# Second attention of a four-layer block: sums stay with heads on partitions, denominators of two units collected, inverted and spread by DMA

## The chip, the cores and the metric

The kernel runs on one core of one Trainium2 chip. The metric is the device time of one execution in microseconds (us), the median of repeated runs. The engines are TensorE (PE: matrix products, transposes through an identity matrix), VectorE (DVE), ScalarE (ACT), GpSimd (POOL) and SyncE (SP), whose queue issues every DMA of this kernel.

## The reference

`x` has 4 batches of 1024 tokens with 256 channels; `ctx` has 77 tokens a batch. Four residual steps follow each other; the change lies in the third.

```python
x = x + tanh(g_xattn[0]) * L0_xattn(layernorm(x), ctx, ...)
x = x + tanh(g_ffn[0])   * L0_ffn(layernorm(x), ...)
x = x + tanh(g_xattn[1]) * L1_xattn(ctx, ctx, layernorm(x), mask, Wv, Wk, Wq, Wo, bo)
x = x + tanh(g_ffn[1])   * L1_ffn(layernorm(x), ...)

def L1_xattn(values, keys, queries, mask, Wv, Wk, Wq, Wo, bo):   # 16 heads of 16 channels
    v, k, q = values @ Wv.T, keys @ Wk.T, queries @ Wq.T         # per head
    energy = where(mask, einsum('bqhd,bkhd->bhqk', q, k), -1e20)
    attn = softmax(energy / sqrt(16), axis=-1)                   # over 77 keys
    out = einsum('bhqk,bkhd->bqhd', attn, v).reshape(N, 1024, 256)
    return out @ Wo.T + bo
```

## The kernel before

The second attention works in 16 **units** `u`: batch `u // 4`, and four heads `4 * (u % 4)` to `4 * (u % 4) + 3`. Each unit has two **steps** of 512 queries, numbered `m = 2 * u + q`, so 32 steps. A step of PE is `scores1(m)`: for each of four heads a product for the row maxima of the next unit (L1278, L1280), then the scores with keys on partitions (L1313, L1314). Then come `values1(m - 1)` (L1322), `max_transposes1(m + 2)` (L1293) and `out_transposes1(m - 2)` (L1331). In the steps m = 2, 4, ..., 16 four transposes of normalised input (L1257) stand among the scores.

`values1` leaves 128 rows in one bank of PSUM: for each of four heads, 32 rows, of which the first 16 are the head's output channels and row 16 is the sum of the exponentials, the softmax denominator. ACT copies the bank to one of two buffers `Oe` (L933), `out_transposes1` turns it so that queries are on partitions, and DVE (`normalise1`) takes the reciprocal of the denominators (L1891) and multiplies (L1894) into `On`. After the 32 steps PE turns `On` back, 512 queries at a time (`transposes1`, L1356), ACT copies that to `OnT` (L957), and PE projects it with `wo1` (L1375). There are eight such chunks `c`. DVE adds each to `x` (`x3_batch`, L1925), takes the statistics of the next normalisation (L1931), and normalises (L1703); then the fourth step's transposes begin (L1388).

Beside it: ACT takes the exponentials of the scores (L945, four a step) and stages the negated maxima (L927); POOL copies those into the query stack (`max_rows1`, L746), which `scores1` of two steps later waits for, and after the steps 20, 23, 26 and 29 adds a bias to one batch of `x` (L763). DVE reduces the maxima (L1872).

SP's queue loads the query stack of each unit three units ahead: `load_x_stack(u)`, six DMAs of 16 partitions with 4 rows of 2 KB each (L541). It waits for the scores of unit u - 3, whose buffer it takes, and the maxima of unit u are the first to read it, from the first product of step 2u - 2. After the loads of u = 2, 5, 7, 9 and 11 it writes chunks of the split input to memory (`write_parts`, L533, 768 KB each), which later loads read. PE waits for ACT (`s_e1`, `s_oc`), for DVE (`s_mr`) and for the loads (`s_xs`); nothing else orders the work but each engine's own list.

Of the kernel before, what the change touches and what calls it, by code (L numbers as in the profile page):

```python
# [11 lines left out]
F32 = mybir.dt.float32  # L12
# [26 lines left out]
def build_program(nc, ins, out):  # L39
    ctx = ExitStack()  # L40
    with ctx:
# [131 lines left out]
        s_fs = sem("ffn0_setup_product")  # L173
        s_fsc = sem("ffn0_setup_copied")
# [36 lines left out]
        Oe = R2f[:, 6100:7124].rearrange("p (u n) -> p u n", u=2)  # L211
# [8 lines left out]
        On = R1[:, :].rearrange("p (i c) -> p i c", i=NT)  # L220
        OnT = R3f[:, 0:2048].rearrange("p (u j n) -> p u j n", u=2, j=2)
        Mn = small[:, 464:496].bitcast(BF16).rearrange("p (u q j) -> p u q j", u=2, q=8)
        rc1 = small[:, 528:544].rearrange("p (q j) -> p q j", q=4)
# [27 lines left out]
        s_ot1 = sem("out1_transposed")  # L251
        s_rc = sem("out1_recip")
        s_on = sem("out1_normalised")
        s_gb = sem("gated_bias")
        s_xb = sem("bias_added")
# [20 lines left out]

        QP = nc.dram_tensor("q_parts", (3, B * C, S), BF16).ap()
# [74 lines left out]
        s_gb2 = sem("gated_bias2")  # L352
        s_xb2 = sem("bias2_added")
# [9 lines left out]
        s_kf = sem("k_copied")  # L363
# [124 lines left out]
        def _(sp):  # L488
# [57 lines left out]
            write_parts(1)  # L546
            for u in range(UNITS):
                b = u // 4
                if u % 4 == 0:
                    sp.wait_ge(s_pw[0], 16 * (b + 1))  # L550
                    sp.wait_ge(s_pw[1], 16 * (b + 1))
                load_x_stack(u)
                for c in WRITES.get(u, ()):
                    write_parts(c)
            sp.wait_ge(s_ksc, 6)
# [3 lines left out]
                         allow_slow_non_contiguous=True).then_inc(s_qgl, 16)  # L559
            def write_qk(dst, c, filled, written):  # L560
# [120 lines left out]
        def _(pool):  # L681
# [100 lines left out]
            pool.tensor_scalar(bp2[:, :], bp2[:, :], gates[:, 3:4], None, ALU.mult).then_inc(s_gb2, 1)  # L782
# [30 lines left out]
            pool.wait_ge(s_gb2, 1)  # L813
            pool.wait_ge(s_xn, 4 * NC)
            for b in range(B):
                xs = X[:, TB * b:TB * b + TB, :]
                pool.tensor_tensor(xs, xs, bp2[:, :].unsqueeze(1).to_broadcast([P, TB, C]), ALU.add).then_inc(s_xb2, 1)
# [6 lines left out]
        def _(act):  # L824
# [25 lines left out]
            for j in range(2):  # L850
                act.wait_ge(s_fs, j + 1)
                act.copy(BWt[:, j, 0:NB16], bank(4 + j)[:, 0:NB16]).then_inc(s_fsc, 1)
            act.wait_ge(s_fs, 3)
            act.copy(BW[0:97, :], bank(6)[0:97, 0:C]).then_inc(s_fsc, 1)
# [97 lines left out]

            for c in range(NC):
                act.wait_ge(s_onT, c + 1)
                if c >= 2:
                    act.wait_ge(s_wo, c - 1)
                act.copy(OnT[:, c % 2], bank(2 * (c % 2), 2).rearrange("p (j t) -> p j t", j=2)).then_inc(s_onc, 1)  # L957
# [89 lines left out]
            for c in range(NC):  # L1047
                n = NC + c
                act.wait_ge(s_onT, n + 1)
# [6 lines left out]
        def _(pe):  # L1056
# [73 lines left out]
            for j in range(2):  # L1130
# [3 lines left out]
                mm.then_inc(s_fs, 1)  # L1134
            pe.wait_ge(s_fsc, 2)
            for j in range(2):
                mm = pe.matmul(bank(6)[0:97, 0:C], BWt[:, j, :], wdT[:, j, :], start=(j == 0), stop=(j == 1))
            mm.then_inc(s_fs, 1)
            pe.wait_ge(s_x1, 4 * B)
            pe.wait_ge(s_fsc, 3)  # L1140
# [185 lines left out]
            def out_transposes1(m):  # L1326
                pe.wait_ge(s_oc, m + 1)
                if m >= 1:
                    pe.wait_ge(s_on, m)
                for i in range(4):  # L1330
                    mm = pe.transpose(bank(3)[:, P * i:P * i + P], Oe[:, m % 2, P * i:P * i + P], identF[:, :])  # L1331
                mm.then_inc(s_ot1, 1)

# [4 lines left out]
            for m in range(2 * UNITS):  # L1338
# [864 lines left out]
```

## Time and profile before

| | |
|---|---|
| median of 3 runs | 1333.91 us (1333.17 to 1338.76) |
| the profiled execution | 1333.7 us, span 1332.0 us |
| PE busy | 1215.1 us, 91% of the span |
| DVE, ACT, POOL busy | 1000.7, 835.3, 227.5 us |
| DMA | 92.55 MB, mean 69 GB/s |
| the 32 steps of the second attention | from about 230 to 383 us of the span |
| its projection | 383 to 421 us |

PE's clock is shown as a share of full speed. The rows further down are of three kinds: stretches of time with the busy time of each engine; the chain of work that ended last, followed back from the end, where an item on the chain delays everything behind it; and timelines. A matmul's printed duration contains its passage through the array, so matmuls overlap; the chain shows what each adds.

### The profile page before, as it was taken

Reading aid. Unit: us, or ns where it says so; the run is one execution under the profiler, and the core shown is the slowest. Engines: PE = TensorE matmul, PEld = TensorE weight load, DVE = VectorE, ACT = ScalarE, POOL = GpSimd, SP = SyncE. Lnnn points to the kernel's source line nnn. Section 1 sums busy time; section 2 is a strip of 40 time slices with the busy share of each in tenths; the row PEclk is TensorE's granted clock in tenths of the full one; section 3 lists DMA queues with packets and bytes.
Section 4 is the critical chain, followed back from the end, with each engine's and each line's share of the span. In section 5 each row is a group of like instructions: output and inputs, shape, how many; then the busy total and the mean of one; then the engine's idle time right before and its main releaser. Section 6 shows DMA issues by size and latency. Waiting matters only on the chain.

```text
span 1332.0 us, 26359 instructions
## 1 busy us (share of the span) xinstructions
PE 1215.1 (91%) x10562; PEld 565.5 (42%) x10562; DVE 1000.7 (75%) x1491; ACT 835.3 (63%) x1484; POOL 227.5 (17%) x176
## 2 busy tenths in 40 slices
PE   4989974999999898879999999999999999999988
PEld 3566762555567455343233232332232333333247
DVE  4895695665536758368999999999999999999602
ACT  1224573777742742115887878887788877888861
POOL 2130124554741423710000000000000000000000
PEclk9878985999999999888999999999999999999989
DMA  6100027557500334722323443144332543233003
GB/s 189 26 1 15 1 31 137 121 108 136 96 1 1 119 119 135 134 35 48 56 62 64 87 72 63 47 82 84 56 68 56 87 78 59 56 70 50 2 1 126
DMA packets 78825, 92.55 MB, mean 69 GB/s; under 512 B 15210, under 2 KB 53356, under 8 KB 78704
## 3 DMA queue, kind: packets, MB, share of 16 engines
q1 hardware_dynamic: 78704, 90.87, 33.7%
q8 instruction: 84, 1.38, 0.5%
q14 instruction: 37, 0.30, 0.1%
HBM read 67.02 MB, written 23.80 MB: 68 GB/s over the span
## 4 chain that ended last, share of the span: by engine, by line
PE 60%; DVE 27%; ACT 5%; issue 2%; SPq 2%; DMA 2%; POOL 1%; DVEq 0%; ACTq 0%; POOLq 0%
DVE sm L2093 19%; PE ps L1560 10%; PE ps L1551 9%; PE ps L1532 6%; ACT W L1022 3%; PE ps L1322 2%; PE ps L1670 2%; PE ps L1416 2%; PE ps L1313 2%; PE ps L1314 2%; PE ps L1375 2%; PE ps L1542 1%; PE ps L1280 1%; PE ps L1278 1%; PE ps L1331 1%
## 5 line engine op out<-in xcount | busy, mean ns | idle before, releaser
L1022 ACT ACTIVATE W<-ps 128x512 f32<-128x512 f32 x1024 | 534.8, 605 | 140.6 <-PE ps L1560 136.7
L2093 DVE TENSOR_REDUCE sm<-ps 128x1 f32<-128x1024 f32 x512 | 599.3, 1217 | 29.7 <-PE ps L1532 26.3
L1560 PE MATMUL ps<-R 99*32 99x512 bf16 x4096 | 319.2, 384 | 5.5 <-ACT W L1022 3.2
L1551 PE MATMUL ps<-W,R 128*32 128x512 f32 x2048 | 265.5, 594 | 0.7 <-ACT W L1022 0.7
L1560 PEld LDWEIGHTS ps<-R 99*32 99x32 bf16 x4096 | 86.1, 94 | 225.2 <-ACT W L1022 167.0
L803 POOL COPY R<-R 128x512 f32<-128x512 f32 x16 | 9.7, 613 | 629.5 <-PE ps L1551 625.9
L1532 PE MATMUL ps<-R 50*128 50x512 bf16 x512 | 89.9, 390 | 17.7 <-DVE sm L2093 15.0
L1532 PE MATMUL ps<-KM,R 50*128 50x512 bf16 x512 | 87.3, 384 | 9.6 <-DVE sm L2093 6.6
L945 ACT ACTIVATE R<-ps 77x512 f32<-77x512 f32 x128 | 75.1, 592 | 23.5 <-PE ps L1314 14.2
L1551 PEld LDWEIGHTS ps<-W,R 128*32 128x32 f32 x2048 | 63.0, 111 | 42.2 <-ACT W L1022 1.4
L1872 DVE TENSOR_REDUCE small<-ps 128x4 bf16<-128x308 f32 x128 | 57.5, 472 | 23.2 <-PE ps L1280 23.1
L746 POOL COPY R<-R 4x2048 bf16<-4x2048 bf16 x32 | 60.5, 1890 | 60.1 <-ACT R L927 54.1
L1532 PEld LDWEIGHTS ps<-R 50*128 50x128 bf16 x512 | 22.2, 93 | 97.0 <-DVE sm L2093 47.2
L1532 PEld LDWEIGHTS ps<-KM,R 50*128 50x128 bf16 x512 | 22.0, 93 | 89.7 <-issue 48.4
L1416 PE MATMUL ps<-R,W 128*128 128x512 f32 x128 | 57.9, 595 | 0.0
L1703 DVE TENSOR_SCALAR XN<-X,mv,rstd 128x256 f32<-128x256 f32 x128 | 46.7, 431 | 9.8 <-PE ps L1092 9.6
L1313 PE MATMUL ps<-R 100*77 100x512 bf16 x128 | 49.0, 383 | 0.0
L1314 PE MATMUL ps<-R 77*77 77x512 bf16 x128 | 48.6, 380 | 0.0
L1891 DVE RECIPROCAL small<-ps 128x16 f32<-128x16 f32 x32 | 8.2, 257 | 47.1 <-PE ps L1331 47.1
L1278 PE MATMUL ps<-R 77*128 77x308 bf16 x128 | 38.7, 303 | 4.1 <-DMA R<-x_parts 4.0
L2104 DVE RECIPROCAL sm<-ps 128x16 f32<-128x16 f32 x32 | 8.2, 257 | 44.7 <-PE ps L1542 44.7
L1280 PEld LDWEIGHTS ps<-R 96*128 96x128 bf16 x512 | 35.0, 100 | 12.9
(262 smaller groups left out, 1576.0 us busy)
## 6 DMA issues: line engine op xcount, KB each, us to landing
R<-x_parts SPq DMA_DIRECT2D x96, 128.0 KB, 4.8
R<-q_parts SPq DMA_DIRECT2D x192, 64.0 KB
R<-q_parts SPq DMA_DIRECT2D x96, 128.0 KB
R<-k_parts SPq DMA_DIRECT2D x96, 128.0 KB
x_parts<-R SPq DMA_DIRECT2D x8, 768.0 KB, 7.0
q_parts<-R SPq DMA_DIRECT2D x24, 256.0 KB, 2.6
k_parts<-R SPq DMA_DIRECT2D x24, 256.0 KB, 2.6
X<-in_x SPq DMA_DIRECT2D x4, 1024.0 KB, 9.8
```

What stands on the lines that cost most here:

```text
L746: pool.tensor_copy(Xs[m // 2 % 3][SR:SR1, :, 512 * (m % 2):512 * (m % 2) + 512], mrow1[:, m % 2].unsqueeze(1).to_broadcast([4, 4, 512])).t ...
L945: act.activation(P1[:, m % 2, j, :], score_bank1(n)[0:KX, :], ACT.Exp, scale=0.25).then_inc(s_e1, 1)
L1022: act.activation(PR[:, s % 2, h, :], third_bank("score", 64 * u + n), ACT.Exp, scale=0.25).then_inc(s_sfree, 1)
L1278: pe.matmul(o, mb1[:, P * q:P * q + P], I4, start=True, stop=False, skip_group_check=True)
L1313: pe.matmul(o, K1s[:, 4 * hg + j, KX * b:KX * b + KX], Xs[u % 3][:, j, t], start=True, stop=False)
L1314: pe.matmul(o, I4[:, 0:KX], mb1[:, t], start=False, stop=True).then_inc(s_sc, 1)
L1416: mm = pe.matmul(o[:, 512 * j:512 * j + 512], wqkv[:, i, C * kind + P * j:C * kind + P * j + P], XNT3[:, i, 512 * c:512 * c + 512], start= ...
L1532: mm = pe.matmul(pl[:, 512 * i:512 * i + 512], QMH[j][h][v, P * q:P * q + P], KM[j][v, h, :], start=True, stop=True)
L1551: mm = pe.matmul(bank(7)[32 * h:32 * h + 32, :], VST[j][:, k, h, :], PR[:, s % 2, h, :], start=(k == 0), stop=(k == TB - 1))
L1560: mm = pe.matmul(o[32 * c:32 * c + 32, :], KST[j][0:MAX_ROW + 1, h, t:t + 32], QST[j][0:MAX_ROW + 1, h, 512 * (s // 8):512 * (s // 8) + 51 ...
L1872: dve.tensor_reduce(Mn[:, u % 2, q, :], bank(n % 2)[:, 0:4 * KX].rearrange("p (j n) -> p j n", j=4), AX, ALU.max, negate=True).then_inc(s_ ...
L2093: dve.tensor_reduce(MX[:, half, h, q:q + 1], bank(2 * ((p + 1) % 2), 2), AX, ALU.max).then_inc(s_tfree, 1)
```

## The change

The sums keep heads on partitions from `values1` to the projection. `out_transposes1`, `normalise1`, `transposes1` and ACT's copies to `OnT` are gone. In their place SP's queue moves things:

- `sort_out1(m)`: ACT's copy in `Oe` (now four buffers) is sorted by four DMAs of 16 partitions x 2 KB into `OT1`, where channels are on partitions in the order that the projection reads, and a fifth DMA puts the four rows of denominators into memory (`DN1`).
- For each **pair** `k` of units (2k and 2k + 1), and each half q: `load_sums1` brings the eight denominator rows back spread over 128 partitions, DVE inverts them (`invert_sums1`), `store_factors1` writes them, and `spread_factors1` brings each row back on 16 partitions. DVE multiplies `OT1` by that (`divide_pair1`). The pairs 5, 6 and 7 are divided behind the loop, the last two between the additions of `x3_batch`.
- The projection reads `OT1` directly and waits for the divided pairs (`s_nd1`).

Some semaphores of other stages are merged or dropped; no instruction of those stages changes.

```diff
-        Oe = R2f[:, 6100:7124].rearrange("p (u n) -> p u n", u=2)
+        Oe = [R2f[:, a:a + 512] for a in (6100, 6612, 7168, 7680)]
...
+        OT1 = R1[:, :].rearrange("p (j b t) -> p j b t", j=2, b=B)
+        Rd1 = R2f[:, 5946:6074].rearrange("p (u q n) -> p u q n", u=2, q=2)
+        Den1 = W[:, 2152:3176].rearrange("p (q n) -> p q n", q=2)
...
+            def sort_out1(m):
+                u, q = m // 2, m % 2
+                b, rows, j = u // 4, 64 * (u % 2), u // 2 % 2
+                sp.wait_ge(s_oc, m + 1)
+                if m >= 2:
+                    sp.wait_ge(s_od1[q], 80 * (m // 2))
+                for h in range(4):
+                    v = slice(rows + 16 * h, rows + 16 * h + 16)
+                    sp.dma_start(OT1[v, j, b, 512 * q:512 * q + 512],
+                                 Oe[m % 4][32 * h:32 * h + 16, :]).then_inc(s_od1[q], 16)
+                sp.dma_start(DN1[u // 2 % 2, q, 4 * (u % 2):4 * (u % 2) + 4],
+                             Oe[m % 4][16:P:32, :]).then_inc(s_od1[q], 16)
+            def load_sums1(k):
+                for q in range(2):
+                    sp.wait_ge(s_od1[q], 80 * (2 * k + 2))
+                    sp.dma_start(Rd1[:, k % 2, q, :],
+                                 DN1[k % 2, q].rearrange("g (a n) -> (g a) n", a=16)).then_inc(s_dd1[q], 16)
+            def store_factors1(k):
+                for q in range(2):
+                    sp.wait_ge(s_ri1, 2 * k + q + 1)
+                    sp.dma_start(DR1[k % 2, q].rearrange("g (a n) -> (g a) n", a=16),
+                                 Rd1[:, k % 2, q, :]).then_inc(s_dd1[q], 16)
+            def spread_factors1(k):
+                for q in range(2):
+                    sp.wait_ge(s_dd1[q], 32 * k + 32 + (16 if k == UNITS // 2 - 2 else 0))
+                    if k >= 1:
+                        sp.wait_ge(s_nd1, 2 * (k - 1) + q + 1)
+                    sp.dma_start(Den1[:, q, :], DR1[k % 2, q].unsqueeze(1).to_broadcast([8, 16, 512])
+                                 ).then_inc(s_db1[q], 16)
+            def store_sums1(u):
+                for m in (2 * u, 2 * u + 1):
+                    sort_out1(m)
+                if u >= 3 and u % 2 == 1:
+                    store_factors1((u - 3) // 2)
+                if u >= 4 and u % 2 == 0:
+                    spread_factors1((u - 4) // 2)
+                if u >= 2 and u % 2 == 0:
+                    load_sums1((u - 2) // 2)
             for u in range(UNITS):
...
+                if u >= 3:
+                    store_sums1(u - 3)
...
+            for u in range(UNITS - 3, UNITS):
+                store_sums1(u)
+            load_sums1(UNITS // 2 - 1)
+            spread_factors1(UNITS // 2 - 2)
+            store_factors1(UNITS // 2 - 1)
+            spread_factors1(UNITS // 2 - 1)
...
             def copy_out1(m):
                 act.wait_ge(s_pv, m + 1)
-                if m >= 2:
-                    act.wait_ge(s_ot1, m - 1)
-                act.copy(Oe[:, m % 2], bank(7)).then_inc(s_oc, 1)
+                if m >= 4:
+                    act.wait_ge(s_od1[m % 2], 80 * (m // 2 - 1))
+                act.copy(Oe[m % 4], bank(7)).then_inc(s_oc, 1)
...
-                if m >= 2:
-                    out_transposes1(m - 2)
             values1(2 * UNITS - 1)
-            out_transposes1(2 * UNITS - 2)
-            out_transposes1(2 * UNITS - 1)
...
             for c in range(NC):
-                if c + 1 < NC:
-                    transposes1(c + 1)
-                pe.wait_ge(s_onc, c + 1)
+                b, q = c // 2, c % 2
+                pe.wait_ge(s_nd1, 4 * b + 3 + q)
...
-                        mm = pe.matmul(o, OnT[:, c % 2, j, P * i:P * i + P], wo1[:, j, :],
+                        mm = pe.matmul(o, OT1[:, j, b, 512 * q + P * i:512 * q + P * i + P], wo1[:, j, :],
...
+            def invert_sums1(k):
+                for q in range(2):
+                    dve.wait_ge(s_dd1[q], 32 * k + 16)
+                    dve.reciprocal(Rd1[:, k % 2, q, :], Rd1[:, k % 2, q, :]).then_inc(s_ri1, 1)
+            def divide_pair1(k, q):
+                dve.wait_ge(s_db1[q], 16 * (k + 1))
+                o = OT1[:, k % 2, k // 2, 512 * q:512 * q + 512]
+                dve.tensor_tensor(o, o, Den1[:, q, :], ALU.mult).then_inc(s_nd1, 1)
...
-                if m >= 2:
-                    normalise1(m - 2)
+                if m >= 9 and m % 4 == 1:
+                    invert_sums1((m - 9) // 4)
+                if m >= 13 and m % 4 in (1, 2):
+                    divide_pair1((m - 13) // 4, m % 4 - 1)
```

How the instructions stand, at three places. First SP's queue, before: two units of loads (`x_parts` is the split input in memory, `R` any of the large buffers).

```order
L541 DMA R<-x_parts 16x4x1024 [waits scores1]
L541 DMA R<-x_parts 16x4x1024 x5
L533 DMA x_parts<-R 128x6x512 [waits part_l]
L541 DMA R<-x_parts 16x4x1024 [waits scores1]
L541 DMA R<-x_parts 16x4x1024 x5
```

The same place of SP's queue with the change, for one unit in which a chunk is written and a pair's factors are spread (`sum_rows` is `DN1`, `sum_factors` is `DR1`).

```order
L541 DMA R<-x_parts 16x4x1024 [waits scores1]
L541 DMA R<-x_parts 16x4x1024 x5
L533 DMA x_parts<-R 128x6x512 [waits part_l]
L555 DMA R<-R 16x512 [waits out1_sorted0,out1_copied]
L555 DMA R<-R 16x512 x3
L557 DMA sum_rows<-R 4x512
L555 DMA R<-R 16x512 [waits out1_sorted1,out1_copied]
L555 DMA R<-R 16x512 x3
L557 DMA sum_rows<-R 4x512
L577 DMA W<-sum_factors 128x1x512 [waits out1_divided,out1_factors_moved0]
L577 DMA W<-sum_factors 128x1x512 [waits out1_divided,out1_factors_moved1]
L563 DMA R<-sum_rows 128x32 [waits out1_sorted0]
```

Between one unit's loads and the next's the queue now holds ten sorting DMAs and either four (here) or two for the factors; the next loads stand behind all of them, and behind their waits. Second, PE behind the last scores, before (`XN` is the normalised input).

```order
L1322 MATMUL ps<-R 32x512 x4
L1331 MATMUL ps<-identF,R 128x128 x8
L1356 MATMUL ps<-identF,R 128x128 x8
L1363 MATMUL ps<-sm 128x2
L1356 MATMUL ps<-identF,R 128x128 x8
L1375 MATMUL ps<-wo,R 128x256 x8
```

PE behind the last scores with the change.

```order
L1360 MATMUL ps<-R 77x512
L1368 MATMUL ps<-R 32x512 x8
L1386 MATMUL ps<-sm 128x2
L1398 MATMUL ps<-wo,R 128x256 x64
L1411 MATMUL ps<-identF,XN 128x128 x16
```

All transposes between the last values and the next stage are gone; the 64 products of the projection follow each other. Third, DVE during the projection with the change (L1914 divides, L1909 inverts, L1947 adds to `x`).

```order
L1914 TENSOR_TENSOR R<-R,W 128x512 [waits out1_factors_spread0]
L1914 TENSOR_TENSOR R<-R,W 128x512 [waits out1_factors_spread1]
L1909 RECIPROCAL R<-R 128x32 [waits out1_factors_moved0]
L1909 RECIPROCAL R<-R 128x32 [waits out1_factors_moved1]
L1940 COPY sm<-ps 128x2 [waits q_g_product]
L1947 SCALAR_TENSOR_TENSOR X<-ps,gates,X 128x1024 [waits biases_added,projected] x2
L1909 RECIPROCAL R<-R 128x32 [waits out1_factors_moved0,x3_added]
L1909 RECIPROCAL R<-R 128x32 [waits out1_factors_moved1]
L1914 TENSOR_TENSOR R<-R,W 128x512 [waits out1_factors_spread0]
L1914 TENSOR_TENSOR R<-R,W 128x512 [waits out1_factors_spread1]
L1953 BN_STATS stats<-X 128x6 x8
```

The statistics of the first batch now stand behind the factors of pair 6, which come through the queue above.

## Rows read from the trace of the kernel before

**Rows 1.** Stretches: us, busy (instructions) of PE, PEld, DVE, ACT, POOL, clock, DMA share, GB/s
```profile
320.00:350.00 30.00, 30.00 (x286) 16.33 (x283) 15.40 (x38) 22.88 (x39) 17.76 (x9) 1.00 0.63 115
```

**Rows 2.** Chain that ended last, one step: start us, us, engine, output, line
```profile
339.99 0.99 PE ps L1322 x8
...
341.21 0.59 PE ps L1331 x4
...
342.08 0.22 PE ps L1313
...
344.67 0.99 PE ps L1322 x8
```

**Rows 3.** The same chain earlier, four transposes among the scores
```profile
300.35 0.44 PE ps L1257 x4
```

**Rows 4.** Timeline of ACT, one step: start us, us, line, operation [idle before]
```profile
304.83 2.69 ACT L945 ACTIVATE R<-ps 77x512 f32<-77x512 f32 x4 [0.37 <-PE ps L1314]
307.95 0.58 ACT L933 COPY R<-ps 128x512 f32<-128x512 f32 x1 [0.43 <-PE ps L1322]
308.56 0.58 ACT L927 CAST R<-ps 4x512 bf16<-4x512 f32 x1
```

**Rows 5.** DVE groups of the whole run: busy us, mean ns | idle before
```profile
L1894 DVE TENSOR_TENSOR R<-ps,small 128x256 f32<-128x256 f32 x32 | 13.6, 424 | 1.1
...
L1821 DVE TENSOR_TENSOR R<-R 128x1024 f32<-128x1024 f32 x8 | 9.8, 1226 | 0.3
...
L1891 DVE RECIPROCAL small<-ps 128x16 f32<-128x16 f32 x32 | 8.2, 257 | 47.1 <-PE ps L1331 47.1
```

**Rows 6.** Timeline, SP's queue: one unit's six loads
```profile
306.92 2.65 SPq L541 DMA_DIRECT2D R<-x_parts  x6
```

**Rows 7.** Stretches of half a us: clock, DMA share, GB/s; loads, then a chunk's write
```profile
311.50:312.00 0.50, 1.00 1.13 139
...
324.50:325.00 0.50, 1.00 1.09 385
```

**Rows 8.** Chain that ended last, the stage's first load: first issue, last issue's landing
```profile
212.02 0.32 SPq L541
...
214.26 6.08 DMA R<-x_parts
```

**Rows 9.** Timeline of POOL around one bias addition
```profile
333.01 1.89 POOL L746 COPY R<-R 4x2048 bf16<-4x2048 bf16 x1 [2.77 <-ACT R L927]
334.98 4.52 POOL L763 TENSOR_TENSOR X<-X,bo 128x2048 f32<-128x2048 f32 x1
```

**Rows 10.** Chain that ended last, from the last values product to the next stage
```profile
382.57 0.60 PE ps L1331 x4
...
387.69 3.72 PE ps L1375 x16
...
392.28 3.46 PE ps L1375 x16
...
413.09 1.29 DVE X L1925
...
414.41 2.71 DVE stats L1931 x8
...
417.88 2.35 DVE XN L1703 x7
...
421.56 1.08 PE ps L1388 x8
```

**Rows 11.** DMA issues of the whole run: count, KB each, us from issue to landing
```profile
q_parts<-R SPq DMA_DIRECT2D x24, 256.0 KB, 2.6
```

**Rows 12.** Timeline of POOL and DVE, later in the kernel
```profile
513.99 2.12 POOL L791 TENSOR_TENSOR R<-R 128x1024 bf16<-128x1024 f32 x1 [3.56 <-ACT R L997]
...
514.25 1.87 DVE L2012 TENSOR_TENSOR sm<-sm 128x1 f32<-128x1 f32 x1
...
517.12 0.19 DVE L2017 TENSOR_TENSOR sm<-sm 128x32 f32<-128x32 f32 x1
```

More of the change, by code:

```diff
@@ L250, in build_program @@
         s_oc = sem("out1_copied")
[L251 to L255, printed above, removed]
+        s_od1 = [sem(f"out1_sorted{n}") for n in range(2)]
+        s_dd1 = [sem(f"out1_factors_moved{n}") for n in range(2)]
+        s_db1 = [sem(f"out1_factors_spread{n}") for n in range(2)]
+        s_ri1 = sem("out1_recip")
+        s_nd1 = sem("out1_divided")
+        s_gb = sem("gated_biases")
+        s_xb = sem("biases_added")
         s_onT = sem("heads_transposed")
@@ L275, in score_bank1 @@
             return bank(4 + n % 3)
+        DN1 = nc.dram_tensor("sum_rows1", (2, 2, 8, 512), F32).ap()
+        DR1 = nc.dram_tensor("sum_factors1", (2, 2, 8, 512), F32).ap()
         QP = nc.dram_tensor("q_parts", (3, B * C, S), BF16).ap()
@@ L850, in _ @@
             for j in range(2):
[L851 to L854, printed above, removed]
+                act.wait_ge(s_ks, 6 + j + 1)
+                act.copy(BWt[:, j, 0:NB16], bank(4 + j)[:, 0:NB16]).then_inc(s_ksc, 1)
+            act.wait_ge(s_ks, 6 + 3)
+            act.copy(BW[0:97, :], bank(6)[0:97, 0:C]).then_inc(s_ksc, 1)
             def y_copy(c):
@@ L951, in _ @@
             copy_out1(2 * UNITS - 1)
[L953 to L957, printed above, removed]
             def transpose_copy(c):
@@ L1324, in values1 @@
                 mm.then_inc(s_pv, 1)
[L1326 to L1332, printed above, removed]
             for q in range(2):
@@ L1343, in _ @@
                     max_transposes1(m + 2)
-                if m >= 2:
-                    out_transposes1(m - 2)
             values1(2 * UNITS - 1)
-            out_transposes1(2 * UNITS - 2)
-            out_transposes1(2 * UNITS - 1)
-            def transposes1(c):
-                if c >= 2:
-                    pe.wait_ge(s_onc, c - 1)
-                for j in range(2):
-                    for i in range(4):
-                        mm = pe.transpose(bank(2 * (c % 2) + j)[:, P * i:P * i + P],
-                                          On[:, 4 * c + i, P * j:P * j + P], identF[:, :])
-                mm.then_inc(s_onT, 1)
-            pe.wait_ge(s_on, 2 * UNITS)
-            transposes1(0)
             pe.wait_ge(s_qc, 2)
@@ L1914, in _ @@
                             blk[:, :].unsqueeze(2).to_broadcast([P, 8, 16])).then_inc(s_qc, 1)
-            normalise1(2 * UNITS - 2)
-            normalise1(2 * UNITS - 1)
+            for q in range(2):
+                divide_pair1(UNITS // 2 - 3, q)
+            invert_sums1(UNITS // 2 - 2)
             dve.wait_ge(s_qk, 1)
@@ L1940, in _ @@
                 x3_batch(b)
+                if b == 0:
+                    invert_sums1(UNITS // 2 - 1)
+                    for q in range(2):
+                        divide_pair1(UNITS // 2 - 2, q)
+                if b == 1:
+                    for q in range(2):
+                        divide_pair1(UNITS // 2 - 1, q)
                 if b + 1 < B:
```

46 lines of the change are left out of this document (13 added, 33 removed).

## The prediction

> **What bounds the kernel now.** I read the stretches first, to see which engine is full in the second attention. PE is busy for all of the 30 us, at clock 1.00, its 2.4 GHz level, while DVE has 15.40, ACT 22.88 and the DMA engines a share of 0.63 [rows 1]. The chain then gives a step's length: from one values product to the next 344.67 - 339.99 = 4.68 us, all of it PE, and 0.59 us of that is the output transposes L1331 [rows 2]. So PE sets the pace, and what it loses is gained until another engine or queue takes over. Three come close.
>
> ACT needs 2.69 + 0.58 + 0.58 = 3.85 us a step [rows 4], under the 4.08 us that PE would have left. SP's queue takes 2.65 us for six DMAs, the first one's 0.32 us shorter than the rest [rows 6, 8]; that is a pitch of (2.65 - 0.32) / 5 = 0.466 us. The DMA engines move a unit's loads at 139 GB/s although their share is full, and a chunk's write at 385 [rows 7]: loads of 16 partitions are slow. From the first issue of a unit's loads to their landing it was 214.26 + 6.08 - 212.02 = 8.3 us [rows 8]. A load may start when its buffer's scores are done and is needed two steps and a bit later (values, maxima, transposes: 342.08 - 339.99 less two small products, 1.8 us), so before it has 9.4 + 1.8 - 8.3 = 2.9 us to spare.
>
> **The change part by part.** The sum is made against the profiled execution, 1333.7 us, which lies 0.2 us under the median.
>
> *PE, in the loop.* 30 times L1331 at 0.59 us [rows 2]: at most 17.7 us, a step of 4.68 - 0.59 = 4.09.
>
> *DVE.* 32 reciprocals of 0.257 and 32 products of 0.424 us go, 21.8 us [rows 5]. 16 reciprocals of twice the width and 16 products of 512 columns come; half of the 1024-column product is 0.61 us, and with 0.26 to 0.51 for a reciprocal this is 14 to 18 us. DVE has half of the stretch free [rows 1], so neither counts, as long as DVE does not wait in line. In the loop it inverts a pair six steps after the pair's last step and divides it four steps later. The load of the sums is issued some four and a half steps after that last step and lands 2.6 us later, by the nearest row for a plain transfer [rows 11]; one step is left. Zero, with that step as cover.
>
> *SP's queue.* Per pair of units (four steps): 12 loads, 20 sorting DMAs, 6 for the factors = 38 x 0.466 = 17.7 us, and 18.1 with a chunk's write. Before, four steps took 18.7 us, or 19.5 with two sets of L1257 at 0.44 us (m = 2 to 16) [rows 3]. PE alone would need 16.3 and 17.2. So the queue, and no longer PE, is the floor: the gain is 1.4 us per four steps for three groups (steps 5 to 16) and 1.0 for 2.75 groups (17 to 27), 6.9 us together; before step 5 and behind step 27 the queue is not full, some five steps gain their 0.59, 3.0 us. In-loop gain **9.9 us** in place of 17.7. The bounds for a sorting DMA's issue are those of the rows: 0.32 us (gain near 17) and 0.466; I take the upper one, as all repeated DMAs of one shape have it.
>
> *POOL.* A bias addition stands between two copies of maxima: 1.89 + 0.08 + 4.52 + 0.1 + 1.89 = 8.5 us from the first copy's start to the second's end [rows 9], and PE reads the second's result at 342.08 [rows 2], 9.1 us after that start. At 4.09 us a step that shrinks to 7.9, late by 0.6 three times; at the queue's 4.42 it is 8.6 and hidden. I take 0.5 us lost, between 0 and 1.8.
>
> *The loads behind the queue.* This is the added wait that matters: the next unit's six loads stand behind the sorting DMAs, whose second set waits for ACT's copy of the last step. From the moment the scores are done: the copy is 4.42 + 1.7 us later, then five issues (2.3) and four for the factors (1.9) = 10.3, against 8.8 for two steps. Every second unit's loads are issued 1.5 us late, with two transfers of 256 KB just ahead of them: 0.7 us each at a write's 385 GB/s, 1.9 at a load's 139 [rows 7]. The spare time has shrunk to 8.8 + 1.2 - 8.3 = 1.7 us. So every second load is late by 1.5 + 1.4 - 1.7 = 1.2 us or more: six times, **7 us lost**. The bounds: 0, if sorts and loads slip past each other, and the case below where the engines are full.
>
> For the rate of a sorting DMA the row at 139 GB/s speaks [rows 7]: it too moves 16 partitions x 2 KB, 0.24 us each. The Trainium skill, SBUF — State Buffer, "Door 1: The DMA port swizzle", says that 16 partitions reach only four of sixteen ports, with 104 GB/s measured; the trace's 139 is above it, and by the page's figure a sort would be an estimated 0.32 us, which makes the rival of full engines dearer by 1.3 us per four steps. The Trainium skill, DMA: Bandwidth & Descriptors, "Rules for kernel authors", says of many small transfers to coalesce them, as under 64 KB one pays mostly overhead; these are 32 KB, and the queue's pitch above is such an overhead. Taken as a forecast, that rule leaves nothing of the in-loop gain: 1333.7 - 5 = 1329 us.
>
> *Behind the loop.* From the last values product's end to the next stage's transposes it is 421.56 - 382.57 = 39.0 us [rows 10]. Gone are the two last turns and divisions with a copy, 387.69 - 382.57 = 5.1 us, and seven times 392.28 - 387.69 - 3.72 = 0.87 us of L1356: PE alone gains 11.2. But pairs 6 and 7 now pass through the queue. From the last values: copy 0.8, five issues 2.3, landing 2.6, sums loaded 0.9 + 2.6, factors spread (pair 6 waits for pair 7's sums by the semaphore's count) 0.9 + 2.6: 12.7. DVE then: two divisions 1.3, statistics 2.71 + 0.6, two additions 2.6, two divisions 1.3 (pair 7 is back by then), statistics 3.3, additions 2.6, statistics 3.3, normalisation 2.35, one addition 1.3: 34.0 us. PE, at 3.46 us a chunk, is done with its part by then. Gain 39.0 - 34.0 = **5.0 us**, between 0 (a landing more in the chain) and 11.2.
>
> Sum: 9.9 - 0.5 - 7 + 5.0 = 7.4; 1333.7 - 7.4 = **1326.3 us**.
>
> **The rivals.**
>
> 1. *The DMA engines fill up* (slower). Where the sorts and the spreading run at the loads' rate, four steps need 2 x 5.7 us for the loads (768 KB at 139), 16 x 0.24, 2 x 1.9, and 2.0 for a chunk: 20.9, and 18.9 without the chunk, against 19.5 and 18.7 before. That is 3 x 1.4 + 2.75 x 0.2 = 4.8 us lost, and a late load idles PE while SP waits for the copy that comes late from it, which I put at 2 us a group, 11.5. With 3.0 and 5.0 gained outside: slower by 8.3, **1342 us**. It decides from some 0.16 us a sort on. For it: the full share at 139 GB/s. Against: the queue issues sorts at a fourth of the loads' bytes per us, much of it into gaps (share 0.63).
> 2. *Late loads take the whole in-loop gain* and the tail stays near 3: **1331 us**, no change that can be told.
> 3. *Everything is hidden*: issues of 0.32 us, loads in time; PE's pace: 17.7 - 1.8 + 5 = 20.9, **1313 us**.
> 4. *A division waits for POOL.* A DVE product of one column with both inputs in SBUF took 1.87 us while POOL's product ran, and ended with it; one of 32 columns later took 0.19 [rows 12]. The divisions are of that kind. The one of step 21 comes as the bias addition of 4.52 us starts [rows 9]; with two maxima ahead in the banks (1.4 us) PE would stand 3.1 us: **1329 us**. In the Trainium skill, SBUF — State Buffer, "Who interferes with whom", this is a rule: a DVE instruction with two SBUF inputs contends with a GpSimd instruction that reads SBUF. The trace agrees.
>
> **How the numbers follow.** A measurement can tell about 0.5%, 6.7 us: under 1327.2 is faster, over 1340.6 slower. The forecast (1319 to 1330) has 0.45, of which a quarter lies above 1327.2; rival 3 has 0.13, rival 2 0.17, rival 4 0.05, rival 1 0.20, a tenth of it under 1340.6. Faster: 0.34 + 0.13 = 0.47; slower 0.18; same 0.35. The range of 1314 to 1341 leaves out half of rival 3 and half of rival 1. The forecast's own range is 1319 to 1330.
>
> **What would show it.** Right: PE waits for the x_parts loads in every second unit; steps of some 4.4 us; SP's issues back to back; the stretch from the last values to L1411 at 34 us. The queue term is wrong if L555 is issued at much under 0.4 us. Rival 1 shows as PE waits of several us and a DMA share near 1.0 throughout; rival 4 as one L1914 of over 3 us. The prediction falls if PE's chain still runs unbroken, or if the tail is longer than 39 us.

## The result: slower by 4%, and the profile after

The changed kernel takes **1388.33 us** (1386.12 to 1390.68, 4 runs) against 1334.03 for the kernel before on the same chip: 1.0401 times as long, 95% interval 1.0375 to 1.0427. The forecast was 1326.3, and the range ended at 1341. The profiled execution took 1388.78 us. Some kernels below had executions over 1.5% longer than their fastest; the ratios leave these out, the medians hold all.

First the stretches of the profile after, cut where the granted clock changes; they answer to [rows 1], where PE was full at 1.00. Columns: stretch, then PE, PE's weight loads, DVE, ACT and POOL busy (instructions), granted clock, DMA share, GB/s.

```profile
243.20:279.40 36.20, 33.29 (x320) 17.78 (x317) 19.42 (x44) 28.72 (x51) 23.24 (x17) 1.00 0.75 129
279.40:286.30 6.90, 6.41 (x32) 3.72 (x32) 2.51 (x5) 2.36 (x4) 1.23 (x3) 0.51 0.43 85
286.30:303.30 17.00, 14.25 (x137) 7.41 (x136) 8.79 (x20) 12.58 (x22) 9.69 (x7) 1.00 0.87 162
303.30:310.20 6.90, 4.22 (x24) 2.93 (x25) 0.96 (x2) 1.61 (x3) 0.74 (x1) 0.51 0.73 130
310.20:327.20 17.00, 15.36 (x146) 7.87 (x144) 8.31 (x17) 13.32 (x24) 10.10 (x8) 1.00 0.79 148
327.20:439.60 112.40, 107.50 (x521) 45.54 (x521) 32.93 (x69) 48.28 (x82) 43.31 (x27) 0.50 0.45 92
...
443.30:473.20 29.90, 26.43 (x122) 22.61 (x120) 24.36 (x73) 0.00 (x0) 6.29 (x7) 1.00 0.14 41
```

The clock falls to 0.5, its 1.2 GHz level, three times. Twice it is back after 6.9 us; the third time, from 327.20 on, it stays there to the loop's end, with PE busy for 107.50 of 112.40 us. What comes before each fall stands in the chain of waits (start us, us, what), here for the first one:

```profile
271.10 1.00 PE ps L1368 x8
...
275.27 1.04 PE ps L1368 x8
...
277.64 1.90 POOL R L798
279.54 0.35 issue
279.89 0.42 PE ps L1324
280.31 0.26 PE ps L1326 x4
```

A step of the unbroken stretch takes 275.27 - 271.10 = 4.17 us, against 4.68 before [rows 2]. Then PE stands from 276.49 to 279.89: L1324 opens the next unit's maxima, behind the wait for that unit's stack. The chain names POOL's copy of maxima, but that copy is for the step after this one, and it ended 0.35 us earlier (the item "issue"); the last packet of the unit's loads landed at 279.80. The other two gaps, 300.55 to 305.98 and 325.56 to 331.30, end 0.1 us behind such a landing too (305.89, 331.21). Behind the third a step takes 7.9 us:

```profile
336.94 1.87 PE ps L1368 x8
...
344.84 1.87 PE ps L1368 x8
```

Why the loads are late stands in SP's own queue (start us, us, what; the issues answer to [rows 6]):

```profile
271.34 2.77 SPq L541 DMA_DIRECT2D R<-x_parts  x6
274.21 2.42 SPq L555 DMA_DIRECT2D R<-R  x4
276.68 0.53 SPq L557 DMA_DIRECT2D sum_rows<-R  x1
277.30 3.70 SPq L555 DMA_DIRECT2D R<-R  x4
281.05 0.52 SPq L557 DMA_DIRECT2D sum_rows<-R  x1
281.61 0.91 SPq L569 DMA_DIRECT2D sum_factors<-R  x2
282.56 2.77 SPq L541 DMA_DIRECT2D R<-x_parts  x6
285.38 0.43 SPq L533 DMA_DIRECT2D x_parts<-R  x1
285.90 3.30 SPq L555 DMA_DIRECT2D R<-R  x4
289.25 0.53 SPq L557 DMA_DIRECT2D sum_rows<-R  x1
289.88 2.41 SPq L555 DMA_DIRECT2D R<-R  x4
292.33 0.52 SPq L557 DMA_DIRECT2D sum_rows<-R  x1
292.89 1.65 SPq L577 DMA_DIRECT2D W<-sum_factors  x2
294.58 0.93 SPq L563 DMA_DIRECT2D R<-sum_rows  x2
295.62 0.36 SPq L541 DMA_DIRECT2D R<-x_parts  x1
```

The queue never stands. Four steps take it 295.62 - 271.34 = 24.3 us, PE alone 4 x 4.17 = 16.7, or a little more with L1303 (the four transposes of normalised input in every second step up to 16, L1257 before). Four sorts take 2.4 us, a pitch of 0.63, and here up to 3.7.

**Where the time went.** From the first values product to the end of the last one it was 143.65 us before (238.92 to 382.57) and is 199.58 (240.07 to 439.65): +55.9. The tail fell from 39.0 to 33.6 us (439.65 to 473.24): -5.4. The rest is +1.2 ahead of the loop and +2.2 behind the tail; the sum is 53.9 = 1385.9 - 1332.0, the difference of the two spans. In the loop the gaps are 3.40 + 5.43 + 5.74 = 14.6 us; the long half-clock stretch costs 107.50 x (1 - 4.17 / 7.89) = 50.7 and the two short ones (6.41 + 4.22) x 0.47 = 5.0. Without these 70.3 us the loop would be 129.3, that is 14.4 shorter than before. So the expected gain is there, and the clock takes nearly four times as much. These terms hang together, though: at half clock PE takes 4 x 7.9 = 31.6 us for four steps, more than the queue's 24.3, so behind the third gap no load was late any more. At full clock more gaps would have come; experiment 4 is such a case.

### The profile page after: what moved, and what is told of

It reads as the page before. It is cut to its first block, busy times and chain, and to the rows that moved or that the text cites. A ratio compares the mean times of both kernels' runs of the same rounds, so it can differ in the third digit from the quotient of the medians.

```text
span 1385.9 us, 26119 instructions
## 1 busy us (share of the span) xinstructions
PE 1253.3 (90%) x10370; PEld 568.4 (41%) x10370; DVE 999.9 (72%) x1459; ACT 827.1 (60%) x1476; POOL 227.5 (16%) x176
## 4 chain that ended last, share of the span: by engine, by line
PE 61%; DVE 27%; ACT 5%; issue 3%; DMA 2%; SPq 2%; POOL 1%; DVEq 0%; ACTq 0%; POOLq 0%
DVE sm L2122 18%; PE ps L1582 10%; PE ps L1573 9%; PE ps L1554 6%; PE ps L1439 3%; ACT W L1068 3%; PE ps L1368 3%; PE ps L1359 3%; PE ps L1360 3%; PE ps L1324 2%; PE ps L1692 2%; PE ps L1326 2%; PE ps L1564 1%; PE ps L1459 1%; PE ps L1447 1%
## 5 line engine op out<-in xcount | busy, mean ns | idle before, releaser
L1894 DVE TENSOR_REDUCE small<-ps 128x4 bf16<-128x308 f32 x128 | 60.4, 477 | 109.7 <-PE ps L1326 109.5
L1324 PE MATMUL ps<-R 77*128 77x308 bf16 x128 | 47.8, 374 | 18.8 <-issue 11.2
L1360 PE MATMUL ps<-R 77*77 77x512 bf16 x128 | 64.4, 503 | 0.0
L1359 PE MATMUL ps<-R 100*77 100x512 bf16 x128 | 64.3, 502 | 0.0
L1326 PEld LDWEIGHTS ps<-R 96*128 96x128 bf16 x512 | 43.7, 120 | 25.0 <-issue 10.7
L1326 PE MATMUL ps<-R 96*128 96x77 bf16 x512 | 49.2, 232 | 0.0
L1368 PE MATMUL ps<-R 77*32 77x512 f32 x256 | 47.2, 819 | 0.8 <-ACT R L985 0.8
```

The lines of the kernel that those rows point to most:

```text
L1324: pe.matmul(o, mb1[:, P * q:P * q + P], I4, start=True, stop=False, skip_group_check=True)
L1326: mm = pe.matmul(o[:, KX * j:KX * j + KX], Xs[u % 3][0:SR, j, P * q:P * q + P], K1s[0:SR, 4 * hg + j, KX * b:KX * b + KX], start=False, st ...
L1359: pe.matmul(o, K1s[:, 4 * hg + j, KX * b:KX * b + KX], Xs[u % 3][:, j, t], start=True, stop=False)
L1360: pe.matmul(o, I4[:, 0:KX], mb1[:, t], start=False, stop=True).then_inc(s_sc, 1)
L1368: mm = pe.matmul(bank(7)[32 * j:32 * j + 32, :], V1a[:, u // 4, 4 * (u % 4) + j, :], P1[:, m % 2, j, :], start=True, stop=True)
```

## The experiments

Two theories at first. *Late loads*: the added DMAs make the loads late, PE idles, and its clock falls behind the gaps. *Missing work*: with the turns gone, PE's work is too thin to hold the clock, gaps or not. Each kernel below is compared with the kernel before on its chip.

**1. No added DMAs.** `sort_out1` and all that follows it are taken out.

```diff
-                if u >= 3:
-                    store_sums1(u - 3)
...
-                if m >= 4:
-                    act.wait_ge(s_od1[m % 2], 80 * (m // 2 - 1))
...
-                if m >= 9 and m % 4 == 1:
-                    invert_sums1((m - 9) // 4)
-                if m >= 13 and m % 4 in (1, 2):
-                    divide_pair1((m - 13) // 4, m % 4 - 1)
```

> The changed kernel without its sorting DMAs, without the DMAs of the sums and factors, and without the reciprocals and divisions that hang on them (the projection reads what lies in its input buffer, so the output is left wrong). What stays of the change: PE without the output transposes, four copy buffers. Theory 'late loads' (the added DMAs make the x_parts loads late, PE idles, and its clock falls behind the gaps): no gap of 3 us in the loop, granted clock 1.00 over the whole loop, a step of 4.1 to 4.2 us, 30 x 0.5 = 15 us gained in the loop and up to 11 behind it: 1305 to 1320 us. Theory 'missing work' (with the transposes gone PE's work is too thin to hold the clock, gaps or not): the clock falls to 0.5 from about step 17 on all the same, 13 steps x 3.7 = 48 us lost: 1350 us or more.

The profiled execution, 1317.8 us (ratio 0.9869, 0.9841 to 0.9897, from two of the four), has no gap over 1.4 us and the full clock:

```profile
243.00:373.20 130.20, 125.27 (x1170) 64.88 (x1168) 61.02 (x134) 104.78 (x184) 86.24 (x53) 1.00 0.58 107
```

Its loop is 133.8 us, 9.9 under before's. So thin steps alone need not lose the clock. But the four executions took 1317.8, 1319.2, 1339.8 and 1341.9 us; no profile shows what the longer two did, and "missing work" was not out yet. PE's waits in this loop come to some 5 us, most of them for POOL's copies of maxima behind the bias additions (us in total, times, longest):

```profile
PE ps L1308 <- POOL R L784: 2.8, 3, 1.3
```

**2. The same DMAs with a 32nd of the bytes.**

```diff
-                    sp.dma_start(OT1[v, j, b, 512 * q:512 * q + 512],
-                                 Oe[m % 4][32 * h:32 * h + 16, :]).then_inc(s_od1[q], 16)
+                    sp.dma_start(OT1[v, j, b, 512 * q:512 * q + 16],
+                                 Oe[m % 4][32 * h:32 * h + 16, 0:16]).then_inc(s_od1[q], 16)
```

> The changed kernel with every sorting DMA cut to 16 of its 512 columns: the same number of DMAs, queue places and waits, a 32nd of the bytes (so the projection's input is incomplete). Theory 'late loads by issue' (SP's queue, with its issues and its waits for ACT's copies, is what holds the loads back): PE's gaps and the half clock stay, 1375 to 1390 us. Theory 'late loads by bytes' (the DMA engines are full): the loads land in time, clock 1.00, 1310 to 1330 us. Theory 'missing work': unchanged at about 1388 us, with no gaps before the clock falls.

1385.3 us (1.0370, 1.0348 to 1.0392), with gaps of 2.87, 5.73 and 4.15 us. The issues are as long as with all the bytes:

```profile
268.24 2.78 SPq L541 DMA_DIRECT2D R<-x_parts  x6
271.12 2.42 SPq L555 DMA_DIRECT2D R<-R  x4
```

So it is the issuing in SP's queue, not what the sorts move.

**3. The sorts without the factors.** The loads, stores and spreading of the sums go, and DVE's two operations with them.

> The changed kernel with the sorting DMAs alone: the loads, stores and spreading of sums and factors, the reciprocals and the divisions are left out (the output is not divided). Per four steps 32 DMAs in place of 38 and no wait for DVE in SP's queue. Theory 'late loads': if the 32 DMAs at some 0.5 to 0.6 us (16 to 19 us against PE's 16.4) and the wait for the last copy are enough, gaps and half clock stay in part, 1350 to 1385 us; if the six factor DMAs tip it over, clock 1.00 and 1310 to 1325 us. Theory 'missing work': half clock without gaps, about 1375 us (the tail is shorter by some 10 us).

1368.2 us (1.0232, 1.0188 to 1.0277): gaps of 1.70, 1.44 and 2.64 us, and 0.50 from 319.80 to the loop's end at 428.46. The 32 issues alone are enough; the smaller gaps cost the same clock. One reason why they are smaller: in the changed kernel the loads before the second and third gap stand right behind two spreadings of 256 KB and landed 8.0 and 9.0 us after their last issue, those before the first gap after 6.1; here, without spreadings, ten units in a row landed after 5.1 to 6.9. So what the spreading moves seems to count, where what the sorts move does not; experiment 7 takes it out.

**4. The turns kept as dummies.**

```diff
                     max_transposes1(m + 2)
+                if m >= 2:
+                    for i in range(4):
+                        pe.transpose(bank(3)[:, P * i:P * i + P], wo1[:, i // 2, P * (i % 2):P * (i % 2) + P], identF[:, :])
```

> The changed kernel, all of it, with four dummy transposes of 128 columns (of a constant, into the bank that the removed ones used) at the removed ones' place in every step from 2 on. Theory 'late loads': the loads are late as before, so gaps of some us stay, but a step then holds turns in f32 as the steps up to 16 do, behind which the clock came back after 7 us; 13 x 3.7 = 48 us of the loss go: about 1340 us (1333 to 1352), with short stretches at 0.5 behind gaps. Theory 'missing work': no stretch at 0.5 at all, and about 1330 to 1338 us. If it is neither of the two, the clock stays at 0.5 and the time is 1390 us or more.

1360.5 us (1.0194, 1.0163 to 1.0226). PE still waits for loads (4.63, 1.69 and 2.00 us), and behind each of these gaps the clock falls, but it returns within 7 us, in the steps without L1303 too:

```profile
303.00:312.60 9.60, 4.97 (x26) 3.12 (x26) 4.22 (x6) 2.29 (x4) 1.89 (x1) 0.64 0.79 129
312.60:333.00 20.40, 18.71 (x178) 10.72 (x177) 9.75 (x22) 14.05 (x25) 11.51 (x8) 1.00 0.74 143
333.00:340.00 7.00, 7.00 (x38) 3.31 (x37) 2.06 (x5) 2.92 (x5) 1.30 (x1) 0.51 0.90 159
340.00:357.00 17.00, 15.00 (x143) 8.38 (x142) 10.66 (x16) 11.25 (x20) 10.10 (x5) 1.00 0.68 147
```

Both theories hold in part: late loads bring the clock down, and here, with the turns back in the steps, it does not stay there. The time is above the 1352 expected. Four steps take SP's queue 22.7 to 25.0 us here too, against the 18.7 that PE needed before; with the clock back behind each fall the loop is still 164.2 us, 20.6 more than before's, and PE's waits for loads sum to 11.0 us in seven gaps. So the queue costs more than the change gains even where the clock returns.

**5. One gap, with and without turns.** This is the plainest pair: kernel 1, with and without dummy turns in the steps from 17 on, and in both twelve tiny DMAs ahead of one unit's loads.

```diff
+                if u == 10:
+                    sp.wait_ge(s_sc, 8 * (u - 2))
+                    for n in range(12):
+                        sp.dma_start(DLY[n:n + 1, :], wo1[0:1, 0, 0:16]).then_inc(s_dly, 16)
                 load_x_stack(u)
```

First the turns without the delay:

> The kernel without the added DMAs, reciprocals and divisions (its runs fell into two groups, 1318 to 1319 and 1340 to 1342 us), with four dummy transposes in the steps from 17 on, where the turns of the normalised input are done. As there, the output is left undivided and unsorted. Theory 'thin work': the upper group is gone, all runs within 0.5% at 1318 + 15 x 0.5 = 1326 us (1322 to 1330). Theory 'queue' alone (the two groups have another cause): two groups stay, some 20 us apart.

1315.5 us, all four between 1312.9 and 1318.9: none near 1340, though four executions of each kernel do not show that the turns are why. The time is below the forecast. The loop is 136.0 us, only 2.2 more than without turns, as the 5 us of PE's waits in it are gone. Then the delay without turns, and with them:

> The same delay of unit 10's loads in the kernel without the added DMAs, reciprocals and divisions (output undivided and unsorted as there), whose steps have no turns of the output. Theory 'plain wait': 1318 + 4 = 1322 us, or 1345 in the upper group. Theory 'gap and clock, no way back' (a step without any turns in f32 does not bring the clock back): one gap of 3 to 4 us, then 0.5 until the loop ends, 11 or 12 steps x 3.7 = 41 to 44 us: 1360 to 1368 us in every run.

> The delayed kernel that lost its clock for 113 us behind one gap of 1.9 us (1365.7 us), with four dummy transposes in the steps from 17 on; output undivided and unsorted as there. One thing is changed: what a step holds for PE. Theory 'gap and clock, no way back without turns': the same gap of about 2 us, and the clock at 0.5 for at most 14 us behind it, 1315.5 + 2 + 7 = 1325 us (1317 to 1330). Theory 'the gap alone decides' (turns don't matter): half clock to the loop's end, 1360 us or more.

Without turns 1365.7 us (1.0238, 1.0222 to 1.0253), with them 1323.9 (0.9911, 0.9884 to 0.9938). One gap each, of 1.94 and 1.49 us; the stretches behind it, of the first kernel and of the second:

```profile
312.50:425.20 112.70, 111.72 (x531) 49.02 (x531) 23.64 (x53) 48.87 (x83) 44.60 (x29) 0.50 0.27 47
425.20:452.70 27.50, 25.92 (x120) 22.48 (x120) 21.57 (x67) 0.00 (x0) 6.10 (x6) 1.00 0.00 1
```

```profile
310.80:321.00 10.20, 10.20 (x55) 5.14 (x53) 2.39 (x5) 3.68 (x7) 2.45 (x2) 0.50 0.67 127
321.00:379.50 58.50, 58.29 (x526) 31.55 (x524) 21.10 (x47) 43.98 (x76) 39.78 (x21) 1.00 0.39 69
```

Both times are in the range of the theory in which the clock needs the turns. The two kernels differ by 41.8 us. Against the same kernels without the delay (1317.8 and 1319.2 for the shorter two executions of experiment 1; 1315.5), the late load costs some 47 us without turns and 8.4 with them. What it is in the turns that brings the clock back is not shown. The same delay in the kernel before:

> The kernel before, with one delay: when unit 10's loads are due, twelve tiny DMAs (64 bytes each) go first in SP's queue, 12 x 0.47 = 5.6 us, against 2.9 us to spare. PE stands once for about 3 us at step 18. Theory 'plain wait' (a gap costs its own length): 1334 + 3 = 1337 us. Theory 'gap and clock' (behind a gap the clock falls to 0.5, and with the turns L1331 in the steps it comes back after some 7 us): 3 + 7 x 0.5 = 6.5 us, 1339 to 1342 us.

1337.5 us (1.0017, 0.9997 to 1.0037). Its gap was only 1.01 us (the twelve issues took 3.47 us, not 5.6) and the clock stayed at 1.00 in the loop, so it says nothing on what a fall costs there. It bears out the time that the loads have to spare, by an estimate 3.47 - 1.01 = 2.5 us; the prediction had 2.9.

**6. Fewer issues, or issues elsewhere.** If SP's queue is all, relieving it should end it. Only the order, then POOL's queue:

> The changed kernel with one change of order in SP's queue: the sorts of a unit's second step are issued one unit later, behind the next loads, so that the queue never waits for ACT's last copy; all 38 DMAs per four steps stay. Theory 'queue by number' (38 issues take 20 to 21 us, more than PE's 16.7): loads still late, gaps and half clock as in the changed kernel, 1375 to 1392 us. Theory 'queue by its waits' (the issues fit, the wait for the copy is what delays the loads): no gaps of 3 us, 1320 to 1345 us.

1384.8 us (1.0375, 1.0343 to 1.0407): so it is not the queue's wait for the last copy, but the time of its issues.

```diff
-                sp.dma_start(OT1[v, j, b, 512 * q:512 * q + 512],
+                pool.dma_start(OT1[v, j, b, 512 * q:512 * q + 512],
```

> The changed kernel with the same sorting and denominator DMAs of every step, issued by POOL from its own queue behind its copy of the maxima, instead of by SP; the memory for the denominators has its own place for each pair. Theory 'queue': SP has 12 loads and 6 factor DMAs per four steps, 9 us, so the loads are in time and the time is that of the kernel with its loads in time, 1310 to 1335 us. If POOL's issues are slow enough to make its copies of maxima late (PE waits for L798's row of this kernel), 1340 us or more, and the loads are in time all the same. Theory of 'bytes on the DMA engines': loads still land late, 1375 us or more.

1391.4 us (1.0385, 1.0314 to 1.0456). SP now stands idle, but a POOL issue takes 0.49 us of POOL's own time, its maxima are late, and PE waits for them (L1326 and L783 are this kernel's first product and copy of the maxima; us in total, times, longest):

```profile
PEld ps L1326 <- POOL R L783: 14.2, 11, 2.6
```

Then one sort per unit:

```diff
-        Oe = [R2f[:, a:a + 512] for a in (6100, 6612, 7168, 7680)]
+        Oe = [R2f[:, a:a + 1024] for a in (6100, 7168)]
...
-                    sp.dma_start(OT1[v, j, b, 512 * q:512 * q + 512],
-                                 Oe[m % 4][32 * h:32 * h + 16, :]).then_inc(s_od1[q], 16)
+                    sp.dma_start(OT1[v, j, b, :], Oe[u % 2][32 * h:32 * h + 16, :]).then_inc(s_od1[u % 2], 16)
```

> The whole computation, with the sorting done once per unit instead of once per step: four DMAs of 16 rows x 1024 columns and one for the denominators, behind the copy of the unit's second step; one load, one store and one spreading per pair, placed ahead of the sorts. Per four steps 12 + 8 + 2 + 3 = 25 DMAs in SP's queue in place of 38. Theory 'queue' (the time of the issues in SP's queue makes the loads late): 12 x 0.47 + 8 x 0.62 + 2 x 0.55 + 3 x 0.6 = 13.5 us per four steps against PE's 16.7, so no gap of 3 us, clock 1.00 in the loop, 1310 to 1325 us. Theory 'thin work' (with the loads in time, PE without the transposes still loses its clock in some executions): the loop without gaps but runs spread over 1315 to 1345 us. If a DMA of twice the bytes takes twice the time to issue, or its bytes count after all, gaps and half clock stay: 1370 us or more.

1384.7 us (1.0383, 1.0318 to 1.0448). The rows of 4 KB issue at the 0.63 us of those of 2 KB, so the queue is relieved: it has idle time. But DVE waits 8.6 us at a reciprocal for the load of the sums, and PE behind it 7.8. With dummy turns in every step it took 1369.9 us. In the profiled execution of that kernel, the longest of four at 1384.3 us, the clock stayed at 0.50 for 43 us behind one gap, with PE busy and four turns in each step (columns as in the first stretches):

```profile
346.00:389.00 43.00, 42.94 (x214) 21.32 (x215) 14.01 (x24) 16.48 (x28) 18.09 (x7) 0.50 0.46 74
```

So turns do not bring the clock back at once every time; behind the other falls in loops with turns in each step it took 7 to 17 us. Putting the reciprocals two steps later, and then a third unit buffer, changed nothing:

> The same with three copy buffers of a unit each, so that a unit's sort is issued a whole unit later, behind loads that are due and after its copies have long ended: no wait for ACT is left in SP's queue in the loop. Theory 'queue': loads issued as soon as their buffer's scores are done, as before the change; no gap over 1.5 us, 1312 to 1322 us, apart from 'thin work', which would spread the runs up to 1345 us. Theory 'bytes on the DMA engines': still gaps, 1350 us or more.

With two buffers 1385.8 us, with three 1384.0 (1.0373, 1.0303 to 1.0443). Here the queue issues each unit's loads when its buffer is free, and it is the transfers that are slow. PE waits for DVE's maxima, which stand behind a reciprocal that waits for the load of the sums. In the waits, in the chain, and in the DMA issues from 292.80 to 295.60 (KB each, median us to landing; 5.1 in the profile after):

```profile
PE ps L1327 <- DVE small L1897: 15.6, 2, 8.4
```

```profile
289.34 13.21 DMA R<-sum_rows
```

```profile
R<-x_parts SPq DMA_DIRECT2D x6, 128.0 KB, 10.0
```

32 KB of sums took 13.21 us; 0.77 us ahead of them the spreading of 512 KB had been issued. So behind the full queue stands a second limit, the DMA engines; that the spreading is what fills them is tested next. With dummy turns this kernel took 1367.9 us (1.0220).

**7. Without the spreading's bytes.** PE spreads the factors, by a product with a 0/1 matrix. First with the reciprocals in that layout, 8 rows x 1024:

> The whole computation in another form: one sort per unit into the sorted layout, three unit buffers, the denominators moved straight into 8 rows on chip, inverted there, and spread to 128 rows by a product with a 0/1 matrix on PE into the bank that the turns had; the division reads that bank. No load, store or spreading DMA: 22 issues per four steps, and 512 KB less per pair for the DMA engines. Theory 'the spreading fills the DMA engines' (in the kernel with three unit buffers the loads were issued in time but took 15 us beside a spreading): loads land in time, no gap over 2 us, 1310 to 1330 us. Theory 'the sorts alone do': gaps of some us and half clock, 1350 us or more.

1429.7 us (1.0713, 1.0689 to 1.0736), and 1417.3 with dummy turns: a reciprocal of this shape takes 6.5 us, and DVE's maxima stand behind it.

```profile
L1895 DVE RECIPROCAL W<-W 8x1024 f32<-8x1024 f32 x6 | 39.2, 6536 | 0.1
```

So reciprocals on 128 rows again, and the factors loaded as 32 KB (against the kernel with three unit buffers):

```diff
-                sp.dma_start(Den1, DR1[k % 2].unsqueeze(1).to_broadcast([8, 16, 1024])).then_inc(s_db1, 16)
+                sp.dma_start(Den1[32 * (k % 2):32 * (k % 2) + 8, :], DR1[k % 2]).then_inc(s_db1[k % 2], 16)
...
+                pe.matmul(bank(SPREAD_BANK1.get((k, q), 3)), Sel1[r:r + 8, :], Den1[r:r + 8, 512 * q:512 * q + 512],
+                          start=True, stop=True).then_inc(s_br1, 1)
```

> The whole computation: three unit buffers and one sort per unit as in that kernel, reciprocals again on 128 rows x 64 columns (the 8 x 1024 ones took 6.5 us each and held VectorE and PE), the factors loaded into 8 rows on chip by a DMA of 32 KB in place of 512 KB, and spread by PE with a 0/1 matrix into the bank of the turns, which the division reads; dummy transposes in two of four steps from 19 on. Theory 'the spreading fills the DMA engines': loads in time, no gap over 2 us, clock 1.00 in the loop: 1315 to 1332 us, faster than both kernels. Theory 'the sorts alone are too many bytes': gaps of 2 us or more with short stretches at 0.5, 1335 to 1360 us.

1340.9 us (1.0041, 1.0021 to 1.0062): the loop is repaired, with one gap of 1.28 us and 3.4 us at half clock. The gap and the clock are those of the first theory, the time lies in the range of the second.

```profile
296.70:300.10 3.40, 3.40 (x19) 2.29 (x18) 1.46 (x3) 1.19 (x2) 0.53 (x1) 0.50 1.05 144
300.10:385.80 85.70, 85.49 (x718) 42.21 (x716) 40.57 (x81) 61.49 (x106) 53.10 (x34) 1.00 0.67 123
```

In the profiled execution, the longest of eight (1346.7 us), the loop is 145.65 us, no shorter than before's, since PE does other work in the turns' place; and its tail is 46.9 us, as its last factors stand behind projections in PE's order and the clock is at 0.50 for another 10 us there. With the 33.6 us of the changed kernel's tail it would come to an estimated 1340.9 - 13.3 = 1327.6. That was not run, so no version here that does the whole computation beats the kernel before.

## Why the prediction was wrong

- *PE's step*: right. 4.09 was forecast for PE alone, 4.17 is measured. Without the DMAs the loop gains 9.9 us, which equals the forecast's in-loop gain by luck: that one came from the queue as the floor. For PE alone it said at most 17.7; 30 x 0.51 is 15.3, and the waits of experiment 1 take some 5 of it.
- *SP's queue*: **the first step that failed**, by its price. "The bounds for a sorting DMA's issue are those of the rows: 0.32 us and 0.466": it is 0.63, over the upper bound. Those rows are loads into 16 rows from memory, and no row of before had a DMA between two places on chip. With what hung behind a transfer, four steps take 24.3 us in place of 18.1: not just under the 18.7 of before, but well over it. Experiment 4, with before's work on PE in the loop and the clock coming back, is 25 us slower than the kernel before.
- *The loads behind the queue*: **the second step that failed**, and the dearer one here. It said "every second load is late by 1.2 us or more: six times, **7 us lost**". The trace has three gaps, 14.6 us, the last of them at step 18. And a late load was charged with its own wait alone. PE's clock falls behind it, and in this loop, from step 17 on, does not come back; that is 55.7 of the 70.3 us lost. Experiment 5 shows it alone: 41.8 us between two kernels with one gap each. No rival held it either.
- *Rival 1*, the full DMA engines, had the right sign and the wrong place: with a 32nd of the sorts' bytes the time stayed (1385.3 us). The engines are the next limit, by the spreading, once the queue is relieved: without its bytes 1367.9 us became 1340.9 (experiments 6 and 7, both with dummy turns).
- *Rival 4*: the divisions took 0.63 to 2.34 us, none over 3. The one of 2.34 began beside a bias addition of 4.52 us and ended 0.55 behind its end, as the rival has it, and PE did not wait for it.
- *POOL* cost PE nothing in the changed kernel, where the steps with bias additions took 7.9 us. At 4.17 us a step, in experiment 1, PE waited 2.8 us for it, over the bound of 1.8.
- *DVE* waited for the sums twice in the loop, 4.4 us in all, where the forecast had left one step to spare.
- *The tail*: 34.0 forecast, 33.6 measured. DVE's 21.3 us came as forecast, operation by operation. From the last values (437.71 + 1.94) to the landing of pair 6's factors it took 12.3 us for 12.7, in part by luck: the last spreading took 4.57 us to land, not 2.6, and the load of the sums 1.80, not 2.6.

```profile
437.71 1.94 PE L1368 MATMUL ps<-R 77*32 77x512 f32 x8 [0.80 <-ACT R L985]
```

```profile
444.77 1.80 DMA R<-sum_rows
...
447.34 4.57 DMA W<-sum_factors
451.91 0.02 issue
451.93 0.69 DVE R L1914
...
464.77 1.29 DVE X L1947
466.06 0.02 issue
466.09 2.71 DVE stats L1953 x8
```

Of the signs named, the waits for the loads, SP's issues back to back and the tail of 34 us came; the steps of 4.4 us did not. None of the signs looked at the clock.

## What to carry to other kernels

Where PE sets the pace, look up what the granted clock does behind each gap that a change may open, and price the gap with it: in this loop one gap of 1.94 us cost some 47. Before taking work out of such a loop, ask which steps brought the clock back; these turns were cheap cover at 0.59 us a step, though no sure one (7 to 43 us until the clock was back). Add up a queue's issues against PE's pace before anything else: here 24.3 us against 16.7. And take the issue time of a DMA from a row of the same kind, source and target; without such a row its upper bound is open (here it was 0.63 / 0.466 = 1.35 times the bound taken).

## What the runs showed of the hardware

- The clock stayed at 0.50 with PE busy for 111.72 of 112.70 us, and came back in the projection behind the loop. With turns in each step it stayed there for 43 us in one execution, with PE busy for 42.94 of them. The Trainium skill, TensorE: Matmul & The Clock Gate, "HAM oscillation — how this bites in real kernels", tells of waits for DMA of some 3 to 5 us that bring the clock down between groups of products; the trace agrees, and shorter gaps were followed by a fall too, of 1.28 us (experiment 7), 1.49 and 1.94 (experiment 5), while those of 1.01 (the kernel before, delayed) and up to 1.3 us (experiment 1) were not. Its section "What's actually happening" has a busy array back at the full clock; here the profile calls PE busy, and it is not back. The measurement decides: the busy share of a profile does not tell whether the clock returns.
- The issue time of a DMA in SP's queue goes by its kind and not by its bytes: 0.63 us for a sort of 16 rows with 64 bytes, 2 KB or 4 KB each, 0.47 for a load of the stack, 0.29 for one row of 64 bytes. The Trainium skill, DMA: Bandwidth & Descriptors, "Rules for kernel authors", says to coalesce small transfers; for the issue time the runs agree (half the sorts at the same time each), for the kernel's time they don't, as the next limit stood close behind.
- A reciprocal on DVE took 6.54 us for 8 rows of 1024 columns, 3.35 for 128 rows of 512, 0.55 for 128 rows of 64 and 0.34 for 128 rows of 32: its time goes by the columns, not by the rows.
